# Layer 1 of a Perceiver-like block: the tail as one stage by batches, and TensorE products that nobody reads in the waits

## What is computed

```python
x = x + _L1_xattn_ref(ctx_1024, _layernorm(x, axis=-1), mask, ...)
x = x + _L1_attn_ref(_layernorm(x, axis=-1), W_qkv, b_qkv)
x = x + _L1_ffn_ref(_layernorm(x, axis=-1), w1, b1, w2, b2)
```

## Time and profile before

| | us |
|---|---|
| median of three runs | 2146.72 (2146.2 to 2150.58) |
| the profiled execution | 2148.47 |
| its span, first to last instruction | 2146.7 |
| mean granted clock of TensorE | 0.957 |

### The profile page before, as it was taken

One profiled execution on the slowest core, in us unless ns is written; L12 is line 12 of the kernel. 1 busy time (PEld: TensorE's weight loads), 2 busy tenths in 40 slices (PEclk: granted clock), 3 DMA queues, 4 the chain that ended last, 5 costly groups with the idle time before them and its releaser, 6 DMA issues. The chain is left out here.

```text
span 2146.7 us, 44080 instructions
## 1 busy us (share of the span) xinstructions
PE 1958.7 (91%) x17806; PEld 1083.0 (50%) x17806; DVE 1584.1 (74%) x2795; ACT 1030.7 (48%) x1454; POOL 652.2 (30%) x687
## 2 busy tenths in 40 slices
PE   6799999999589879999999999999999999667898
PEld 2455555555445433555555555555555555433643
DVE  5689999999757764777777777777777776545676
ACT  2689998998713632333333333333333343201453
POOL 3244454454312410223333333332333332122000
PEclk9899999999699889999999999999999999988899
DMA  4323332331242210000000000000000000120400
GB/s 148 99 65 85 99 76 75 99 87 46 57 171 81 79 40 22 22 22 23 22 23 23 22 4 20 22 23 22 22 23 23 22 2 2 50 74 0 152 11 20
DMA packets 40138, 106.16 MB, mean 49 GB/s; under 512 B 19328, under 2 KB 21632, under 8 KB 33792
## 3 DMA queue, kind: packets, MB, share of 16 engines
q1 hardware_dynamic: 39936, 103.35, 15.7%
HBM read 75.42 MB, written 1.05 MB: 36 GB/s over the span
## 5 line engine op out<-in xcount | busy, mean ns | idle before, releaser
L1469 POOL TENSOR_SCALAR a1c_p_hi<-a1c_pf 128x512 f16<-128x512 f32 x272 | 201.4, 741 | 665.1 <-ACT a1c_pf L1525 622.7
L1331 PE MATMUL PS<-a_x_hi,w_next 128*128 128x512 f16 x1088 | 280.1, 380 | 6.0 <-POOL a1c_v_lo L1459 3.6
L1341 PE MATMUL PS<-w_next,a_x_hi 128*128 128x512 f16 x1088 | 279.1, 379 | 0.0
L1494 ACT ACTIVATE a1c_k_hi<-PS 128x512 f16<-128x512 f32 x136 | 81.2, 597 | 326.9 <-PE PS L1331 326.9
L392 POOL TENSOR_SCALAR a0c_p_hi<-a0c_r 128x1024 f16<-128x1024 f32 x128 | 154.9, 1210 | 268.6 <-DVE a0c_r L492 265.7
L1501 ACT ACTIVATE a1c_v_hi<-PS 128x512 f16<-128x512 f32 x136 | 81.5, 599 | 259.0 <-PE PS L1341 206.2
L497 DVE TENSOR_TENSOR a0c_p_lo<-a0c_r,a0c_p_hi 128x1024 f16<-128x1024 f32 x128 | 201.6, 1575 | 0.9 <-POOL a0c_p_hi L392 0.9
L1674 DVE TENSOR_TENSOR a1c_p_lo<-a1c_pf,a1c_p_hi 128x512 f16<-128x512 f32 x272 | 198.1, 730 | 5.2 <-POOL a1c_p_hi L1469 5.2
L1525 ACT ACTIVATE a1c_pf<-PS,a_maskc 128x512 f32<-128x512 f32 x256 | 174.9, 685 | 47.9 <-PE PS L1836 38.3
L1617 DVE CUSTOM_DVE_ANT_0 a1c_junk<-PS,a1c_maskr 128x512 bf16<-128x512 f32 x256 | 175.7, 686 | 18.8 <-DVE a1c_ctop L1617 0.5
L492 DVE TENSOR_TENSOR a0c_r<-PS,a0c_r 128x1024 f32<-128x1024 f32 x128 | 155.3, 1213 | 32.8 <-ACT a0c_r L438 32.6
(11 more groups left out here) (362 smaller groups left out, 4550.2 us busy)
## 6 DMA issues: line engine op xcount, KB each, us to landing
a_cf<-in_ctxT SPq DMA_DIRECT2D x16, 1024.0 KB, 5.2
a0c_ks<-a0c_k_hi SPq DMA_DIRECT2D x128, 128.0 KB, 2.3
a1c_cf<-in_ctx SPq DMA_DIRECT2D x16, 1024.0 KB, 4.8
a0c_ks<-a0c_k_lo SPq DMA_DIRECT2D x64, 128.0 KB, 2.4
f_w<-in_w SPq DMA_DIRECT2D x4, 1024.0 KB, 8.6
f_w<-in_w SPq DMA_DIRECT2D x1, 4096.0 KB, 19.5
s1q_w<-in_L1a_wT SPq DMA_DIRECT2D x3, 1024.0 KB, 7.6
qw_raw<-in_w_gate SPq DMA_DIRECT2D x1, 2816.0 KB, 9.1
```

The source lines that it names most:

```text
L1331: mm = nc.tensor.matmul(out, wk[i][:, k, f * P:(f + 1) * P], (x_hi, x_lo)[j][e][:, k, :], start=(step == 0), stop=(step == 11))
L1341: mm = nc.tensor.matmul(out, (x_hi, x_lo)[j][e][:, k, t * P:(t + 1) * P], wv[i][:, k, group * BANK:(group + 1) * BANK], start=(step == 0), ...
L1469: nc.gpsimd.tensor_scalar(p_hi[:, v % 4, :], pf[:, v % 2, :], 1.0, 0.0, ALU.mult, ALU.add)\
```

## The change

Products that nobody reads: a helper multiplies the 128x128 identity in bfloat16 by itself, n times, into bank 7 of PSUM. It is called in `layer_norm` where it makes zT (32 after the first statistics, 3 between the batches' turns, 24 after the last), in `add_product` (3 between the turns, 12 after them), in the block that divides layer 0's attention (60), at the end of the block of the queries (40, after ScalarE's last cast).

The tail: `transpose_rows`, the blocks `a1o` and `self_attention_1` are replaced by one block, `latents_tail`, in which TensorE goes through the batches one after another: turn and output product for each, then turn of z and projection for each with the turn of the rotated q and k of the batch before, then the attention's steps as they were. Both normalisations are done per batch on VectorE with a root each on ScalarE. ScalarE alone copies the turned tiles, and k into its blocks. The last addition to x goes to GpSimd. z has two buffers, raw and rot two each. The output weight and the columns of the projection for q and k are loaded into the memory of `g.next` by SP at the end of the loop's block, after its last projection; the v columns come in the new block. ScalarE touches Sqrt and Exp once ahead of their use. The semaphores are cleared once instead of twice.

In the diff lines left out are marked; taken out whole are `transpose_rows`, the old blocks and `self_attention_1`. The functions of scores, transposes and outputs of the attention, of bias and rotation and of the normalisation keep their operations, with new names of semaphores and banks.

```diff
             if zT is not None:
                 @block.tensor
                 def _(pe):
+                    pe.wait_ge(stats_done, 1)
+                    idle_matmuls(nc, g, 32)
                     for b in range(B):
                         pe.wait_ge(z_done, b + 1)
                         for k in range(KT):
@@ -164,39 +166,19 @@
                                                     z[:, b, k * P:(k + 1) * P], g.ident[:])
                             if b == B - 1:
                                 t.then_inc(turned, 1)
+                        idle_matmuls(nc, g, 3 if b < B - 1 else 24)
+
+
+def idle_matmuls(nc, g, n, bank=7):
+
+    for _ in range(n):
+        nc.tensor.matmul(g.PS[:, bank, 0:P], g.identb[:], g.identb[:], start=True, stop=True)
 
 
...
@@ -215,6 +197,7 @@
                         t = nc.tensor.transpose(g.PS[:, k, b * P:(b + 1) * P], a[:, b, k * P:(k + 1) * P],
                                                 g.ident[:])
                     t.then_inc(turned, 1)
+                    idle_matmuls(nc, g, 3 if k < KT - 1 else 12)
 
                 pe.wait_ge(loaded, 32)
                 pe.wait_ge(copied_a, 2)
...
                               (bo[:], d["L0x_bo"].broadcast_to([P, D]), out_loaded)])
+                @block.tensor
+                def _(pe):
+                    pe.wait_ge(rec_done, 1)
+                    idle_matmuls(nc, g, 60)
...
     with ExitStack() as ctx:
-        m_ = Memory(nc, ctx, "a1")
+        acc = Memory(nc, ctx, "a1").sb("acc", [P, B, H, W])
+        weights_in = Memory(nc, ctx, "a1").sem("weights_in")
+        wo, wqk = [g.next[:, 2 * i:2 * i + 2, :].rearrange("p i n -> p (i n)").bitcast(F32) for i in range(2)]
+        wo, wqk = wo.rearrange("p (k n) -> p k n", k=FT), wqk.rearrange("p (k n) -> p k n", k=KT)
...
                                                   start=(k == 0), stop=(k == KT - 1))
                         mm.then_inc(product, 1)
+                    pe.wait_ge(hi_done, FT)
+                    idle_matmuls(nc, g, 40)
...
                         tops(j, 1)
                         tops(j + 1, 0)
                         load_context(j + 2)
+                    sp.wait_ge(v_product, 8 * NJ)
+                    sp.dma_start(wo, d["L1x_wo"].rearrange("p (k n) -> p k n", k=FT)).then_inc(weights_in, 16)
+                    sp.dma_start(wqk, d["L1a_wT"].rearrange("p (k n) -> p k n", k=KT)[:, :, 0:2 * D]).then_inc(weights_in, 16)
+                    sp.wait_ge(weights_in, 32)
 
...
+        loop.close()
+        latents_tail(nc, g, d, acc, wo, wqk, weights_in)
+def latents_tail(nc, g, d, acc, wo, wqk, weights_in):
...
+            @block.sync
+            def _(sp):
+                sp.dma_start(bo[:], d["L1x_bo"].broadcast_to([P, D])).then_inc(rows_in, 16)
+                sp.dma_start(go[:], d["L1x_go"].broadcast_to([P, D])).then_inc(rows_in, 16)
+                sp.dma_start(bias[:], d["L1a_b"].broadcast_to([P, 3 * D])).then_inc(rows_in, 16)
+                sp.dma_start(cs[:], d["cos"]).then_inc(rows_in, 16)
+                sp.dma_start(sn[:], d["sin"]).then_inc(rows_in, 16)
+                sp.dma_start(wv[:], d["L1a_wT"].rearrange("p (k n) -> p k n", k=KT)[:, :, 2 * D:3 * D]).then_inc(wv_in, 16)
+            @block.gpsimd
+            def _(pool):
+                nc.gpsimd.memset(warm[:], 0.0).then_inc(warmed, 1)
+                nc.gpsimd.memset(v[:, :, :, W - 1:W], 1.0).then_inc(ones_set, 1)
+                nc.gpsimd.memset(kd[:], 0.0).then_inc(cleared, 1)
+                pool.wait_ge(rows_in, 80)
+                for b in range(B):
+                    pool.wait_ge(based, 3 * b + 2)
+                    rotate(pool, nc.gpsimd, 1, b, k_parts, k_rot)
+                for i in range(2 * B):
+                    b, cols = i // 2, slice(256 * (i % 2), 256 * (i % 2) + 256)
+                    pool.wait_ge(x_done, b + 1)
+                    pool.wait_ge(y_done, i + 1)
+                    nc.gpsimd.tensor_tensor(g.x[:, b, cols], g.x[:, b, cols], y[:, i, :], ALU.add).then_inc(final, 1)
...
+                def turn_a(b):
+                    pe.wait_ge(a_done, b + 1)
+                    if b >= 1:
+                        pe.wait_ge(aT_done, 2 * b)
+                    for half in range(2):
+                        for k in range(KT):
+                            f = KT * half + k
+                            t = nc.tensor.transpose(g.PS[:, half, k * P:(k + 1) * P], a[:, b, f * P:(f + 1) * P], g.ident[:])
+                        t.then_inc(a_turned, 1)
+                def out_product(b):
+                    pe.wait_ge(aT_done, 2 * (b + 1))
+                    if b == 0:
+                        pe.wait_ge(weights_in, 16)
+                    if b >= 2:
+                        pe.wait_ge(o_done, b - 1)
+                    for k in range(FT):
+                        mm = nc.tensor.matmul(g.PS[:, 3 + b % 2, :], aT[:, k, tokens(b)], wo[:, k, :],
+                                              start=(k == 0), stop=(k == FT - 1))
+                    mm.then_inc(product, 1)
+                def turn_z(b):
+                    pe.wait_ge(z_done, b + 1)
+                    if b >= 2:
+                        pe.wait_ge(based, 3 * (b - 1))
+                    for k in range(KT):
+                        t = nc.tensor.transpose(g.PS[:, RING[(3 * b + 2) % 6], k * P:(k + 1) * P],
+                                                z[:, b % 2, k * P:(k + 1) * P], g.ident[:])
+                    t.then_inc(z_turned, 1)
+                def project(b):
+                    pe.wait_ge(zT_done, b + 1)
+                    for i in range(3):
+                        n = 3 * b + i
+                        if n == 0:
+                            pe.wait_ge(weights_in, 32)
+                        if n == 2:
+                            pe.wait_ge(wv_in, 16)
+                        if n >= 6:
+                            pe.wait_ge(based, n - 5)
+                        for k in range(KT):
+                            right = wv[:, k, :] if i == 2 else wqk[:, k, i * D:(i + 1) * D]
+                            mm = nc.tensor.matmul(g.PS[:, RING[n % 6], :], zT[:, k, tokens(b)], right,
+                                                  start=(k == 0), stop=(k == KT - 1))
+                        mm.then_inc(projected, 1)
...
+                def turn_rotated(b):
+                    if b == 0:
+                        pe.wait_ge(o_done, B)
                     for i in range(2):
+                        pe.wait_ge((q_rot, k_rot)[i], 2 * (b + 1))
+                        if b >= 1:
+                            pe.wait_ge((q_out, k_out)[i], (b, HG * b)[i])
                         for f in range(KT):
+                            t = nc.tensor.transpose(g.PS[:, 3 + i, f * P:(f + 1) * P],
+                                                    rot[:, i, b % 2, f * P:(f + 1) * P], g.ident[:])
+                        t.then_inc((q_turned, k_turned)[i], 1)
...
+                idle_matmuls(nc, g, 30)
+                for b in range(B):
+                    turn_a(b)
+                    if b == 0:
+                        idle_matmuls(nc, g, 12)
+                    out_product(b)
+                for b in range(B):
+                    turn_z(b)
+                    project(b)
+                    if b >= 1:
+                        turn_rotated(b - 1)
+                score(0)
+                score(1)
+                pe.wait_ge(based, 10)
+                idle_matmuls(nc, g, 40, bank=0)
+                turn_rotated(B - 1)
+                for n in range(2, N + 4):
+                    if n < N:
+                        score(n)
+                    if n < N + 2:
+                        turn_p(n - 2)
+                    if n >= 4:
+                        output(n - 4)
...
+                def copy_rotated(b):
+                    act.wait_ge(q_turned, b + 1)
+                    nc.scalar.activation(qT[:, :, tokens(b)], g.PS[:, 3, :].rearrange("p (k n) -> p k n", k=KT), ACT.Copy,
+                                         scale=DH ** -0.5).then_inc(q_out, 1)
+                    act.wait_ge(k_turned, b + 1)
+                    if b == 0:
+                        act.wait_ge(cleared, 1)
+                    for h in range(HG):
+                        r = slice(h * DH, (h + 1) * DH)
+                        nc.scalar.copy(kd[r, b, :, h * P:(h + 1) * P], g.PS[r, 4, :].rearrange("p (k n) -> p k n", k=KT))\
+                            .then_inc(k_out, 1)
...
+                copy_a(0)
+                for b in range(B):
+                    copy_o(b)
+                    if b + 1 < B:
+                        copy_a(b + 1)
+                    else:
+                        copy_z(0)
+                    roots(b)
+                act.wait_ge(warmed, 2)
+                nc.scalar.activation(warm[:], warm[:], ACT.Exp).then_inc(warmed, 1)
+                for b in range(1, B):
+                    copy_z(b)
+                    copy_rotated(b - 1)
```

(38 more changed lines are left out.)

434 lines of the change are left out of this document (179 added, 255 removed).

## The result

The changed kernel took 2115.86 us, the median of four executions (2112.94 to 2116.53), against 2147.89 (2146.2 to 2150.58) for the kernel before beside it: ratio 0.9847, 95% interval 0.983 to 0.9864. A second set, run to have a base for the experiments, gave 2114.37 and 0.9844 (0.9826 to 0.9861). The forecast was 2111 in a range of 2103 to 2123: the direction and nine tenths of the size. The profiled execution took 2115.48 with a span of 2113.3, 33.4 less than before.

What follows compares the result with a forecast made beforehand. Stage order bounds the tail, TensorE's 2.19 us pitch the attention loop, the lower clock comes second. Tail 31.0 plus other stages 5.1 make 36.1 off 2146.72: 2110.6, about 2111, range 2103 to 2123.

Steps and rivals of the forecast that it cites:

- A: Tail's start: thirty products 3.2 us at the lower clock, turn 1.7, first output product 6.0 us after the block's start.
- B: Tail's output product: four batches of 6.86 us with three gaps of 1.8 between them, ending at 38.8.
- C: Tail's first z: turn, copy of o and copy of z take 1.35 us, to 40.2.
- D: Tail's projections: four of 10.3 us, a gap of 1.3, then two of 3.85; sum 50.2, to 90.4.
- E: Tail's last turn: two scores, forty products and two turns take 5.8 us, to 96.2; about 1.6 is loss.
- F: Tail's attention: 16 steps at 2.19 us, 33.4 in all, plus startup waits 0.7 and last division and addition 1.9, to 132.2.
- port rival: New tail: divisions blocked beside GpSimd's clear (+4 to 5 us), or projection gaps of 6; say 2120, chance 0.18.
- The rival with the clock down through the whole tail: Tail: TensorE at the lower clock because of gaps between batches; about 2216 if throughout, just past no gain 2155; chance 0.02.
- Item 2: Layer 0's output: sixty products hidden in TensorE's wait, turns and products then at full clock: -3.2 us (-3.6 to 0).
- Items 5 and 6: Before the queries, products start at full clock, -2.0 us; query stage, forty products end late on the path, +1.9.
- Item 7: Before the last layer: unread products let its first products run at full clock, -1.9 us (-3 to 0).
- Rival "filling pays nothing": All stages: unread products don't lift the clock in time or end late; tail gains 28, say 2118; chance 0.22.

Runs made afterwards that it cites:

- only the tail's own products: Changed kernel with the products that nobody reads left out everywhere but in the tail: 2120.35 us, ratio 0.9876.
- the early mask: Changed kernel, linear attention's causal mask loaded one block earlier, behind the v weights: 2111.09 us, ratio 0.9831.
- the old tail: Kernel before with its old tail, plus the unread products at all places outside the tail: 2148.50 us, ratio 0.9993.
- the pair under the new tail: Changed kernel run again (2114.37 us) against the same with unread products only in the tail (2120.35): 6.9 us by ratios, uncertain by 5.3.
- the late weights: Changed kernel, output weight and q and k columns loaded at the start of the tail's block, not the loop block's end: 2122.09 us, ratio 0.9897.
- z first: Changed kernel, next batch's z turned and copied before the previous batch's rotated q and k in the tail: 2109.55 us, ratio 0.9817.

## Why the prediction held, step by step

*Tail.* It was to take 132.2 us and a clock's fall of 1.5; it took 132.5 (1853.06 to 1985.55), the fall of 1.7 in the fourth projection included. A: the first product began 3.7 us after the block's start, not 6.0. What failed here is the 3.2 us for thirty products at the lower level: the loop had left the clock up, they took 1.83 and were over when the first a was ready, and the turn took 1.09 instead of 1.7. This is no rule. The clock was up at that point in seven of the twelve profiles of the new tail; in the kernels with only the tail's own products and with the early mask it was down, and there the forecast of A was right to 0.3: 3.36 us for the thirty and the first product at 5.8.

```profile
1850.97 3.36 PE L175 MATMUL PS<-g_identb 128*128 128x128 bf16 x30 [0.79 <-PEq L1390]
1854.13 1.92 PE L1990 MATMUL PS<-g_ident,lt_a 128*128 128x128 f32 x8
```

B: pitch 8.79 (8.7 forecast). C: the first projection at 38.4, 1.8 earlier than forecast, from the 2.3 of A less some tenths of B. D: pitches 11.7, 14.6, 14.6 (11.6 and 14.2), end at 91.3 (90.4): a gap was 0.4 longer, and the fall lies in here. E: 5.7 (5.8), but the loss of 1.6 in it wasn't one; the step had asked when ScalarE could copy k's turn, and overlooked the two exponentials that stand first. F: 2.19 a step as forecast, end 132.5 (132.2). The divisions beside GpSimd's clear kept their 4.63, so that part of the port rival fell, as the second pair of the earlier trace rows had said; its other part, gaps of 6 us, fell too. Clearing: 0.5 (0.4).

```profile
1853.15 6.95 POOL L1969 MEMSET lt_kd<- 128x8192 f32 x1
...
1853.65 4.63 DVE L2176 TENSOR_TENSOR lt_a<-a_acc,lt_rec 128x1024 f32<-128x1024 f32 x4
```

That the tail came out within 1 us is in part luck: in this profile A was 2.3 short and D 2.7 long, and with the clock as the two other kernels had it the same code took 3.8 us more.

*Clock.* The forecast took a little under one stretch of 2.2 us for the two gaps; in the two profiles of the changed kernel one gap of the two was followed by a fall, and in two others with this order; in five more both were. The one stretch that was priced is thus the low end. The rival with the clock down through the whole tail did not occur: 0.97 to 1.00 here, and a mean of 0.93 or more over the tail in every profile of the new one.

*Other stages.* Item 1: +1.15 (0.7). Item 2: -3.3 (-3.2). Item 3: -0.8 (-0.6). Item 4: +0.5 (0). Items 5 and 6: -0.5 (-0.1), with the forty at 1.7 (1.9). Item 7: -2.9 in this one profile (-1.9); over the profiles the kernels with these products took 126.1 to 128.0 from there to the end and those without 127.1 to 129.2, so it is 1.5 on average, and the two overlap. The sum of 5.1 is the term that was too large: the stages gave 1.4, the old tail's pair at most 3.4, and 2 to 3 is what the two comparisons share, while the pair under the new tail (6.9, uncertain by 5.3) does not exclude 5.1. What was missing are two effects behind the edited places: the mask, for which VectorE waits 0.3 to 2 us longer, and the loop's start. There the prediction did ask where the clock falls, called full clock in the first products hidden, and stopped; that the fall then comes later, on the path, is what it overlooked.

*Rival "filling pays nothing"*: its 2118 is 2 above the measurement, the forecast 5 below it. The rival's number was the nearer one. The result can't tell them apart; the runs show that the products do pay (at least 1.6 us under the new tail), but less than was forecast under the old one.

## To carry to other kernels

When stages of different engines are chained by batches, price the new stage by what each engine does in its own order: here the two waits of 2.7 us that were left stood in ScalarE's list, and putting z's copy ahead of k's gave 7.4 us. Work that only keeps the clock up is worth what the next useful instructions gain, and it also moves everything behind it: look for what else sits near the edge of a wait. An edit worth 2 us is read from the same stage in several profiles, or from medians with their interval, never from two spans.

## What the runs showed of the hardware

*The lower clock can last for 50 us under a busy TensorE.* In the profiled execution of the kernel with the late weights (2144.58 us) the clock fell in linear attention, which its edit does not touch. VectorE had waited 3.89 us for the mask and TensorE, behind it, 1.50; 2.7 us after TensorE went on, the clock fell to 0.50 and stayed there for 51.2 us (665.1 to 716.3). Windows of that kernel, then the nearest of the changed kernel:

```profile
650.00:658.00 8.00, 7.03 (x17) 2.85 (x15) 6.33 (x7) 0.00 (x0) 0.00 (x0) 1.00 0.00 0
...
672.00:690.00 18.00, 18.00 (x53) 12.32 (x53) 5.12 (x13) 7.86 (x11) 6.79 (x11) 0.50 0.40 159
690.00:711.00 21.00, 19.61 (x66) 14.82 (x64) 7.48 (x23) 0.00 (x0) 0.00 (x0) 0.50 0.01 2
```

```profile
673.00:690.00 17.00, 16.29 (x101) 12.35 (x100) 11.44 (x33) 7.87 (x11) 6.79 (x11) 1.00 0.43 167
```

A step of this stage took 3.41 us instead of 1.75, with TensorE busy throughout, and the stage 21.6 us more. In the changed kernel a wait of 3.86 at the same place was followed by full clock, so the wait alone does not decide it; what does stays open. Executions 18 to 30 us above their kernel's others were seen in four kernels, all with the unread products outside the tail and the mask at its old place (8 of their 30 executions). The three other kernels that have both (the changed one, z first, the old tail) showed none in 24 executions, and the five of the changed kernels that lack one or the other none in 21. The mean clock of all eight was 0.959 to 0.962 where the other executions of the same kernels had 0.966 to 0.974, and 51 us at half the clock are 0.012 of 2140; with one such profile it is still only likely that all are this. The Trainium skill (TensorE: Matmul & The Clock Gate, Part 1, its caveats on traces) says that the clock's trace events were found unreliable and that the gate has been seen stuck for 50 us and more, at a quarter of the clock. The trace agrees on the length and not on the level, which is 0.50 here; and the instructions' own durations doubled for that time, so the stretch is real and not a fault of the record.

*The same products raise the clock in one profile and not yet in another*: in the kernel with the old tail 32 of them before the last layer ran 3.60 us at the lower level, and the first transposes behind them still did (1.06 for four, and 1.06 for the next four); in the profile after it was 3.54 us, and the clock was up at the first transpose (0.61 for four). TensorE had stood 2.83 us before them in the one and 3.78 in the other.
